# VectorE adds the sums of two groups back ahead of its product kq in an edge attention kernel

## What is computed

```python
Qh = (x @ Wq.T + bq).reshape(n, H, D)          # n = 6250, H = 4, D = 16
Kh = (x @ Wk.T + bk).reshape(n, H, D)
Vh = (x @ Wv.T + bv).reshape(n, H, D)
Ee = (edge_attr @ We.T + be).reshape(-1, H, D)
score = (Kh[src] * Qh[dst] * (1.0 / np.sqrt(D)) * Ee).sum(-1)
score = jnp.exp(jnp.clip(score, -5.0, 5.0))
msg = Vh[src] * score[..., None]
wV = jax.ops.segment_sum(msg, dst, num_segments=n)
x = _layernorm(x + wV.reshape(n, H * D), axis=-1)
```

## Time and profile before

| | us |
|---|---|
| median of 3 runs | 1672.18 (1670.16 to 1672.41) |
| the profiled execution, its own time | 1674.01 |
| its span, first to last instruction | 1671.8 |
| TensorE matmuls busy | 1574.8 |
| VectorE busy | 1439.3 |
| GpSimd busy | 1220.7 |
| ScalarE busy | 944.4 |

### The profile page before, as it was taken

The page is one execution under the profiler, slowest core; times in us unless marked ns, Lnnn a source line. Parts: engine busy times, 40 slices in busy tenths (PEclk is TensorE's granted clock), DMA queues, the critical chain, the costliest instruction groups (busy, mean ns, idle before and its releaser), DMA issues. The chain is left out here.

```text
span 1671.8 us, 57996 instructions
## 1 busy us (share of the span) xinstructions
PE 1574.8 (94%) x18014; PEld 1394.3 (83%) x18014; DVE 1439.3 (86%) x2549; ACT 944.4 (56%) x2857; POOL 1220.7 (73%) x1298
## 2 busy tenths in 40 slices
PE   5399999999999999999999999999999999999994
PEld 5288888888888888888888888888888888888884
DVE  7389888889889889889889889889889889889886
ACT  3355555555555555555555555555555556556553
POOL 5577777777777777777777777777777777777772
PEclk9599999999999999999999999999999999999995
DMA  9455555555555555555555455555555555455541
GB/s 286 145 141 138 144 140 137 143 141 137 138 145 139 135 146 141 135 145 141 135 144 143 135 141 146 134 139 147 136 136 150 136 135 150 135 137 149 135 126 50
DMA packets 197529, 236.34 MB, mean 141 GB/s; under 512 B 95865, under 2 KB 122593, under 8 KB 197313
## 3 DMA queue, kind: packets, MB, share of 16 engines
q1 hardware_dynamic: 156992, 152.99, 32.7%
q0 software_dynamic: 40512, 83.05, 20.5%
HBM read 228.46 MB, written 7.40 MB: 141 GB/s over the span
## 5 line engine op out<-in xcount | busy, mean ns | idle before, releaser
L283 POOL DMA_INDIRECT kv<-kv_table,idx x1266 | 1203.4, 951 | 410.5 <-issue 388.5
L689 PE MATMUL xg_bank<-x_hi,src_onehot 128*128 128x448 f32 x2422 | 903.3, 373 | 16.7 <-DVE src_onehot L827 10.4
L690 PE MATMUL xg_bank<-x_lo,src_onehot 128*128 128x448 f32 x2422 | 883.6, 365 | 0.0
L689 PEld LDWEIGHTS xg_bank<-x_hi,src_onehot 128*128 128x128 f32 x2422 | 454.9, 188 | 77.0 <-issue 15.3
L690 PEld LDWEIGHTS xg_bank<-x_lo,src_onehot 128*128 128x128 f32 x2422 | 455.4, 188 | 33.2
L766 ACT ACTIVATE distance<-iota_w,dst_neg 128x64 f32<-128x64 f32 x1612 | 428.7, 340 | 0.0
L827 DVE TENSOR_TENSOR src_onehot<-r_row,xg_bank 128x896 fp32r<-128x896 f32 x346 | 372.8, 1077 | 16.0 <-DMA r_row<-r_table 16.0
L839 DVE SCALAR_TENSOR_TENSOR x_sel<-iota_v,src_block,xg_bank 128x448 f32<-128x448 f32 x346 | 233.8, 676 | 23.9 <-PE xg_bank L690 20.2
L792 ACT COPY xg_t_sb<-turn_sum 128x128 f32<-128x128 f32 x198 | 53.0, 268 | 349.1 <-PE turn_sum L699 349.1
L845 DVE TENSOR_REDUCE xg_sb<-x_sel 128x64 f32<-128x448 f32 x346 | 214.4, 620 | 11.9
L871 DVE TENSOR_TENSOR kq<-kv,edge_ps 128x512 f32<-128x512 f32 x202 | 138.2, 684 | 95.3 <-ACT kv L799 92.3
(11 more groups left out here) (111 smaller groups left out, 904.4 us busy)
## 6 DMA issues: line engine op xcount, KB each, us to landing
attr_sb<-attr SPq DMA_DIRECT2D x201, 256.0 KB
dst_row<-dst_rows SPq DMA_DIRECT2D x402, 128.0 KB
kv<-kv_table,idx POOLq DMA_INDIRECT x1266
r_row<-r_table SPq DMA_DIRECT2D x148, 128.0 KB
q_win<-q_table SPq DMA_DIRECT2D x404, 24.0 KB
idx<-src_tab SPq DMA_DIRECT2D x206, 4.0 KB, 4.3
r_row<-r_table SPq DMA_DIRECT2D x50, 64.0 KB
kv_table<-kv_stage SPq DMA_DIRECT2D x7, 448.0 KB, 4.2
```

The lines of the kernel that those rows point to most:

```text
L283: pool.indirect_dma_start(out=kv[:, slot, t, :], out_offset=None, in_=kv_table, in_offset=bass.IndirectOffsetOnAxis(ap=idx[:, slot, t:t + ...
L689: pe.matmul(xg, src_onehot[:, parity, u, :], x_hi[:, u, :], start=(u == 0), stop=False)
L690: mm = pe.matmul(xg, src_onehot[:, parity, u, :], x_lo[:, u, :], start=False, stop=(u == U - 1))
```

## The change

In VectorE's step, both additions of group g - 2, with the read of the window's start, move from their places behind kq and behind kqe to a place ahead of kq. There they stand behind the wait pe_kv_made, which tells that ScalarE has copied the projected rows of the group, and ahead of the waits for the gathered rows (kv_gathered) and for the rows Q (qe_made). In groups without made tiles (0, 1, 200, 201) there is no wait pe_kv_made. The set of instructions stays the same.

```diff
                         slot, n = j, 2 * pairs_of(g)
-                        dve.wait_ge(kv_gathered[slot], 16 * gathered(slot, i))
                         if pe_tiles(g, slot):
                             dve.wait_ge(pe_kv_made, g - (PE_FROM - 1))
+                        if not (isinstance(g, int) and g < 2):
+                            nodes = add_sums(g - 2, (slot - 2) % SLOTS)
+                            add_odd_sums(g - 2, (slot - 2) % SLOTS, nodes)
+                        dve.wait_ge(kv_gathered[slot], 16 * gathered(slot, i))
                         dve.wait_ge(qe_made, 2 * (g + 1))
                         dve.tensor_tensor(by_half(kq[:, 0:n, :]), by_half(kv[:, slot, 0:n, 0:F]), edge_pairs(slot, 1, n),
                                           ALU.mult).then_inc(kq_made, 1)
-                        if not (isinstance(g, int) and g < 2):
-                            nodes = add_sums(g - 2, (slot - 2) % SLOTS)
                         dve.wait_ge(kq_made, g + 1)
                         dve.wait_ge(ee_made, 2 * (g + 1))
                         dve.tensor_tensor(by_half(kqe[:, 0:n, :]), by_half(kq[:, 0:n, :]), edge_pairs(slot, 0, n),
                                           ALU.mult).then_inc(kqe_made, 1)
-                        if not (isinstance(g, int) and g < 2):
-                            add_odd_sums(g - 2, (slot - 2) % SLOTS, nodes)
                         dve.wait_ge(kqe_made, g + 1)
```

## The result

The changed kernel takes 1801.7 us (median of 4 runs, 1796.9 to 1802.5) against 1672.3 us: a ratio of 1.0775, 95% interval 1.076 to 1.0789. It is slower by 129 us, where 105 were forecast. The profiled execution has a span of 1800.3 us.

The account below looks back on a forecast made before the run. TensorE was the bound in name, with VectorE's way from kq to L845 equal to it in three steps of four. 1674.0 + 107 - 3 = 1778 profiled, given as 1777 us for the median; range 1738 to 1820.

Parts of the forecast that it names:

- The register read: VectorE's read of the window's start, behind the wait in slots 0 to 2: 0.78 us, bounds 0.70 and 0.90.
- The order: On VectorE, both additions, kq, kqe, then L882 in dependent pairs: 1.93 us to L882, bounds 1.83 and 2.08.
- the rival in which it costs nothing: Dependent pairs on VectorE cost nothing extra: a turn grows by 0.7 us, 1704 us in all; chance 5%.
- Per slot: Delays by slot after slack: 0.79 us in 0, 0.21 in 1, 0.82 in 2, 0.36 in 3; together 2.18.
- T0: TensorE's turn (L699) in the step of slot 0, others numbered likewise by slot; forecast to start 0.79 us later.
- 49 turns, +107 us: The loop of four-group turns: each grows by 2.18 to 33.6 us, +107 us in all, bounds +75 and +154.
- The end of the loop: Behind the last gather_x, TensorE's waits for the odd half shrink: 3 us gained, bounds 0 and 9.
- The clock: Rival: TensorE's clock falls in its longer waits, once each loop turn, giving above 2100 us; chance 3%.
- The signs: Expected in the profile: "issue" idle ahead of L854, L699's wait near 110 us, clock 1.00, L678's wait gone.
- work without a gap: VectorE from kq of slot 2 to kq of slot 3: claimed continuously busy for 6.59 us, with no slack.
- The no-change rival: TensorE's pace, 94% busy against VectorE's 86%, hides the added time: 1672 us; chance 6%.
- slip into the idle time: Rival: VectorE does the additions and read in the idle 0.5 us ahead of kq: about 1638 us; chance 3%.

Follow-up runs that it names:

- e12: Changed kernel plus 11 and 5 matmuls that nobody reads, in TensorE's waits of slots 3 and 0; 1776.4 us, ratio 1.0631.
- e8: Kernel before with only the register read moved, behind the wait for the projected rows and ahead of kq; 1715.5 against 1670.0 us.
- e7: Changed kernel with the register read ahead of the wait for the projected rows, additions still behind it; 1689.0 against 1670.0 us.
- e9: Kernel before with the register read ahead of the wait for the projected rows, additions in their old places; 1651.5 against 1670.0 us.
- e11: The changed kernel run once more without further edits, against the kernel before; 1799.7 against 1672.0 us, ratio 1.0763.
- the first five runs: Early runs of four edited kernels, one of them twice, where the kernel before took 2968 to 3007 us; ratios 0.9908 to 1.0326.

## Why the prediction was right, and where it fell short

The direction and the mechanism held; the time of 1777 us was 25 us short of 1801.7, inside the range. The 25 us are the clock. Without its falls (e12) the changed kernel takes 1776.4 us, what was forecast; that it fits to a microsecond is in part luck, as single terms below are off both ways.

- *The register read, 0.78 us from kq's old start.* Measured 0.96 us after the copy's end, less the 0.2 that kq took to start: 0.76. e8 shows it alone: 0.75. The row's 0.303 us for the load was the right one to go by (0.312 after).
- *The order, 1.93 us from the first addition to the sum.* Measured 1.95 and 1.94, with steps of 0.25, 0.26, 0.72 and 0.72. The order does cost 0.37 us against the 1.57 of the earlier trace rows, and e7 and e9, which differ in nothing but the place of the additions, show it in the time; so the rival in which it costs nothing falls. That dependence is the reason is shown in part only. kq behind L861 needs nothing of it and still starts 0.26 us later, where L882 starts 0.14 us behind L861 in the old order. The prediction put this piece down to the queue's two more waits. And in the old order L861 starts 0.71 us behind kqe, of which it needs nothing:

```profile
820.01 0.67 DVE L877 TENSOR_TENSOR kqe<-kq,edge_ps 128x512 f32<-128x512 f32 x1
820.72 0.22 DVE L861 TENSOR_TENSOR acc<-acc,turn_sum 64x64 f32 x1
```

So at least 0.12 of the 0.37 us have another cause than dependence, and no run separates the causes.
- *Per slot: T0 0.79, T1 0.21, the way through slots 2 and 3 0.82 + 0.36.* Measured 0.78 for T0, 0.06 for T1 plus 0.14 for T1 to T2, and 1.08 for T2 to T3; in the other kind of turn T0 is 0.91 and T1 0.21 later. The 0.14 is a wait for src_onehot that the prediction had in no slot (21.2 us in the list, of which one wait of 10.6 at the start was there before too, as 10.4). Together 2.06 in this turn, and 33.6 us was the mean turn of e12, against 33.6 forecast.
- *49 turns, +107 us.* With the clock out of play (e12) the first and the last L699 lie 1651.6 us apart, before 1544.3: +107.3.
- *The end of the loop, 3 us.* Behind the last L699 the profiled execution takes 38.3 us, where it took 41.4: 3.1 us are given back. The loop grew by 1676.0 - 1544.3 = 131.7 us and the span by 128.5. But the wait L678 for L861 is not gone, as I said it would be; 6.6 us in 5 waits are left of 9.1.
- *The clock.* This is the step that failed: a term put at nothing in the sum. I had seen the wait of 1.5 us ahead of T3 and given a fall 3%, because it was shorter than the one of 1.7 us before the fall at 1632 and stood between stretches of full work. That was no reason, only a distance from the one fall that the trace had. And I priced it as a case of its own, with a fall in each turn (over 2100 us), where it was a term to add to the forecast: 19 falls in 49 turns, 23 us. With it the sum is 1777 + 23 = 1800.
- *The signs.* I said that "issue" would be named for the idle time; the profile names the copy in 125 groups and "issue" in 25. The start of L849 in the queue's rows told the two apart. TensorE's wait at L699 grew to 97.0 us, not to about 110, and the granted clock did not stay at 1.00.
- *A gap that I overlooked.* I called VectorE's way from kq of slot 2 at 812.70 to 819.29 work without a gap. It has one, ahead of the first addition, for the very read in question:

```profile
813.64 0.21 DVE L854 TENSOR_TENSOR acc<-acc,turn_sum 64x64 f32 x1 [0.25 <-issue]
```

That gap lies on the way that sets T3, and e9 takes it out. Two side sums were off as well, neither of them in the forecast: 0.18 us in each of three slots are 26 us over the run, not about 20; and with pairs that cost nothing a waiting slot grows by 0.78 + 1.57 - 1.89 = 0.46 us, not 0.37, which puts that rival near 1713 us and not at 1704.

The no-change rival, that TensorE's pace hides the loss, was wrong for the reason given: the slack, not the busy share, counts. The additions did not slip into the idle time, as pe_kv_made, the wait ahead of them, is the one that ends last.

## What to carry to other kernels

A register read from memory costs far more time than its instruction, here 0.75 us for a load of 0.3 us, and behind a wait on which the engine stands idle it is paid in full, since the queue works in order. Where the engine is behind its queue (slot 3 here) it costs nothing. Put it ahead of the wait (e9: 18.5 us for one moved line). For a kernel in which two engines feed each other, work out the ring from signal to signal and compare it with the pace of the busier engine; what a change adds to the ring counts in full where the slack is zero. Look beyond the ring too: once it is faster, the next engine (here GpSimd's gathers, 31.3 us a turn) is close behind. And when a change makes TensorE's waits longer (here from 0.5 to 1.5 us), price the clock as a term of its own, since it comes on top.

## What the runs showed of the hardware

- TensorE's clock fell from 2.4 to 1.2 GHz in 19 stretches (85 us) in the kernel with waits of some 1.5 us once a turn (each fall behind one of 1.49 to 1.54 us; the same kernel again, e11, had 19 falls too), and in none inside the loop with waits of up to 1.0 us (e7, e8) or with the same waits filled to 0.4 us at most (e12). Not each of the long waits brings a fall: 19 in 49. Filling them with needless matmuls gave 23 us.
- All comparisons but the first five runs agree within 0.2% on the kernel before (1670.0 to 1672.9 us); in those five the same kernel took 1.8 times as long, on a chip with the number of the one that took 1672.0 us over an hour later (e11, e12).
- Starts on VectorE: behind a product of 0.69 us an addition that doesn't need it starts 0.60 us later, the next product that needs it 0.72 us; behind an addition of 0.21 us it is 0.14 us for an operation that doesn't need it in the old order, and 0.25 us for L861 and 0.26 us for kq in the new one.
